# Ranks of a batch's tokens inside a Mixture-of-Experts router: sums along the tiles by VectorE's shifted additions, not by seven identity products on TensorE

## The reference

```python
logits = x @ wr.T                                  # x: 16384 tokens, 8 experts
vals, idx = jax.lax.top_k(logits, 2)
cap = int((T * 2 // E) * 1.25)                     # 5120
mask = (idx[:, :, None] == jnp.arange(E)).any(axis=1)
pos = jnp.cumsum(mask.astype(jnp.int32), axis=0) - 1   # rank of a token with its expert
keep = mask & (pos < cap)
slot = jnp.where(keep, pos, cap)
dispatch[e, slot] = token                          # then gather, two matmuls per expert, weighted sum
```

## Time and profile before

| What | Value |
|---|---|
| Median of 3 runs | 2128.93 us (2125.66 to 2129.43) |
| The profiled execution | 2128.42 us |
| Its span, from the first to the last instruction | 2126.7 us |
| Mean granted TensorE clock | 0.979 |
| Busy share of the span: PE, DVE, ACT, POOL | 95%, 70%, 58%, 59% |
| Runs of `rank` in the profile | 16, from 81.24 to 551.50 us |

### The profile page before, as it was taken

The page is one execution under the profiler, slowest core; times in us unless marked ns, Lnnn a source line. Parts: engine busy times, 40 slices in busy tenths (PEclk is TensorE's granted clock), DMA queues, the critical chain, the costliest instruction groups (busy, mean ns, idle before and its releaser), DMA issues.

```text
span 2126.7 us, 51586 instructions
## 1 busy us (share of the span) xinstructions
PE 2012.0 (95%) x16208; PEld 1954.1 (92%) x16209; DVE 1484.2 (70%) x4388; ACT 1228.6 (58%) x2775; POOL 1258.0 (59%) x1336
## 2 busy tenths in 40 slices
PE   6999999998269999999999999999999999999997
PEld 5988888887169999999999999999999999999997
DVE  3777887877447667667667767676677676666666
ACT  3566666666345656555656566555556565655654
POOL 1277667776745556565555565466565555655655
PEclk9999999999579999999999999999999999999999
DMA  5234334332222112111211211131131212211221
GB/s 184 80 131 147 126 130 149 121 124 101 71 97 89 42 41 90 50 51 38 89 55 47 96 54 53 47 103 57 53 103 60 65 58 67 66 61 62 74 69 58
DMA packets 102434, 173.11 MB, mean 81 GB/s; under 512 B 26499, under 2 KB 70622, under 8 KB 102256
## 3 DMA queue, kind: packets, MB, share of 16 engines
q0 software_dynamic: 45584, 84.59, 13.0%
q1 hardware_dynamic: 56800, 88.00, 12.1%
HBM read 121.41 MB, written 69.21 MB: 90 GB/s over the span
## 4 chain that ended last, share of the span: by engine, by line
PE 59%; issue 6%; POOL 3%; DVE 2%; DMA 1%; DVEq 1%; POOLq 0%
PE y_ps L1383 29%; PE h_ps L1367 27%; PE tb_ps L1348 2%; POOL rows L1099 1%; DMA out<-y,put_idx 1%; POOL base L1112 1%; POOL rstd_b L1105 1%; POOL out L1120 1%; DVE h_lo L1292 0%; DVE y_raw L1239 0%; DVE y L1272 0%; DVEq L1047 0%; DVEq L1048 0%; DVE w_hi L1309 0%; DVE stats_b L1250 0%
## 5 line engine op out<-in xcount | busy, mean ns | idle before, releaser
L1193 ACT ACTIVATE h_ps<-h_ps,b_sb 128x256 f32<-128x256 f32 x1032 | 415.8, 445 | 595.3 <-PE h_ps L1367 595.3
L1383 PE MATMUL y_ps<-w_hi,h_hi 128*128 128x256 f32 x2064 | 590.0, 286 | 8.5 <-DVE h_lo L1292 8.1
L1367 PE MATMUL h_ps<-bt_hi,w_hi 128*128 128x256 f32 x2064 | 573.4, 278 | 3.4 <-issue 2.0
L1383 PE MATMUL y_ps<-w_hi,h_lo 128*128 128x256 f32 x2064 | 575.9, 279 | 0.0
L1383 PE MATMUL y_ps<-w_lo,h_hi 128*128 128x256 f32 x2064 | 575.4, 279 | 0.0
L1367 PE MATMUL h_ps<-bt_lo,w_hi 128*128 128x256 f32 x2064 | 572.1, 277 | 0.0
L1367 PE MATMUL h_ps<-bt_hi,w_lo 128*128 128x256 f32 x2064 | 571.9, 277 | 0.0
L1383 PEld LDWEIGHTS y_ps<-w_hi,h_hi 128*128 128x128 f32 x2064 | 389.9, 189 | 14.8 <-DVE h_lo L1292 14.5
L1367 PEld LDWEIGHTS h_ps<-bt_hi,w_hi 128*128 128x128 f32 x2064 | 389.2, 189 | 5.2 <-issue 3.4
L1292 DVE TENSOR_TENSOR h_lo<-h_ps,h_hi 128x512 fp32r<-128x512 f32 x516 | 344.6, 682 | 66.8 <-ACT h_hi L1196 66.7
L1383 PEld LDWEIGHTS y_ps<-w_hi,h_lo 128*128 128x128 f32 x2064 | 389.3, 189 | 0.0
(11 more groups left out here) (211 smaller groups left out, 3404.9 us busy)
## 6 DMA issues: line engine op xcount, KB each, us to landing
xt_raw<-in_x_t SPq DMA_DIRECT2D x32, 512.0 KB
x_raw<-in_x SPq DMA_DIRECT2D x64, 256.0 KB, 3.2
w_raw<-in_w SPq DMA_DIRECT2D x16, 1024.0 KB
x_rows<-x_sb SPq DMA_DIRECT2D x32, 512.0 KB
out<-alone SPq DMA_DIRECT2D x32, 512.0 KB
rows<-x_rows,pick_idx POOLq DMA_INDIRECT x260
out<-y,put_idx POOLq DMA_INDIRECT x260, 2.5
base<-out,base_idx POOLq DMA_INDIRECT x258
```

Source lines behind the costliest of these rows:

```text
L1193: nc.scalar.activation(half, half, ACT.Gelu_apprx_tanh, bias=b1_sb[:, bass.ds(e * FT + 2 * g + i, 1)]).then_inc(gelu_done, 1)
L1367: ins = nc.tensor.matmul(h_ps[:, g, (f % 2) * BLK:(f % 2 + 1) * BLK], w[:, c:c + P], v[:, k, :], start=(i == 0), stop=(i == 3 * DK - 1))
L1383: ins = nc.tensor.matmul(y_ps[:, t, :], v[:, g, h:h + P], w[:, c:c + D], start=(f == 0 and t == 0 and part == 0), stop=(f == FT - 1 and t ...
```

## The change

The seven identity products are taken out of `rank`. VectorE instead sums the choices along the 8 tiles of a partition, by three additions at distances of 1, 2 and 4 tiles. The tile `chosen` has four planes with 4 zeroed tiles ahead of the 8 real ones, so that the shifted reads need no special case. The last tile of the last plane is the sum over all 8 tiles, which took a reduction before. A fourth new addition, `ahead_of`, adds the running slot numbers to the sums of the earlier tiles, and `ranked` adds TensorE's rank to that. GpSimd clears `chosen` once at the start, ahead of `minus_half`, and VectorE rounds two matrices to fp32r instead of three.

```diff
+            HEAD = 4
+            chosen = sb("chosen", [P, 4, HEAD + TILES, E])
+            ahead_of = sb("ahead_of", [P, TILES, E])
...
+                made(nc.gpsimd.memset(chosen[:, :, :, :], 0.0))
...
-                for src, dst in ((ident, ident_r), (tri_f, tri_r), (ones_f, ones_r)):
+                for src, dst in ((tri_f, tri_r), (ones_f, ones_r)):
...
-                ROUTE_STEPS = 25
+                ROUTE_STEPS = 28
...
-                        step(V.tensor_tensor(mask[:, :, :], pick[:, 0, :, :], pick[:, 1, :, :], ALU.add))
-                        step(V.tensor_reduce(mask_sum_f[:, :], mask[:, :, :].bitcast(F).rearrange("p t e -> p e t"), X, ALU.add))
-                        V.tensor_copy(mask_sum[:, :], mask_sum_f[:, :]).then_inc(mask_ready, 1)
+                        step(V.tensor_tensor(chosen[:, 0, HEAD:, :], pick[:, 0, :, :], pick[:, 1, :, :], ALU.add))
+                        for i in range(3):
+                            span = 1 << i
+                            step(V.tensor_tensor(chosen[:, i + 1, HEAD:, :], chosen[:, i, HEAD:, :],
+                                                 chosen[:, i, HEAD - span:HEAD - span + TILES, :], ALU.add))
+                        V.tensor_copy(mask_sum[:, :], chosen[:, 3, HEAD + TILES - 1, :]).then_inc(mask_ready, 1)
+                        step(V.tensor_tensor(ahead_of[:, :, :], chosen[:, 3, HEAD - 1:HEAD - 1 + TILES, :],
+                                             over_tiles(slot_next[:, :]), ALU.add))
                         step(V.tensor_tensor(gap[:, :], top[:, 1, :], top[:, 0, :], ALU.subtract))
...
-                        step(V.tensor_tensor(slot[:, :, :], rank_ps, over_tiles(slot_next[:, :]), ALU.add))
+                        step(V.tensor_tensor(slot[:, :, :], rank_ps, ahead_of[:, :, :], ALU.add))
...
-                    nc.tensor.matmul(rank_ps, tri_r[:, :], mask_sum[:, :].rearrange("p (a e) -> p a e", a=1).broadcast_to([P, TILES, E]),
-                                     start=True, stop=False)
-                    for t in range(TILES - 1):
-                        ins = nc.tensor.matmul(rank_ps[:, t + 1:TILES, :], ident_r[:, :],
-                                               mask[:, t:t + 1, :].broadcast_to([P, TILES - 1 - t, E]),
-                                               start=False, stop=(t == TILES - 2))
+                    ins = nc.tensor.matmul(rank_ps, tri_r[:, :], mask_sum[:, :].rearrange("p (a e) -> p a e", a=1).broadcast_to([P, TILES, E]),
+                                           start=True, stop=True)
```

More of the change, by code:

```diff
@@ L130, in build @@
             tri_f, ones_f = sb("tri_f", [P, P]), sb("ones_f", [P, P])
-            ident_r, tri_r, ones_r = sb("ident_r", [P, P], R), sb("tri_r", [P, P], R), sb("ones_r", [P, P], R)
+            tri_r, ones_r = sb("tri_r", [P, P], R), sb("ones_r", [P, P], R)
             second = sb("second", [P, TILES, E])
@@ L138, in build @@
             best = sb("best", [P, TILES])
-            mask = sb("mask", [P, TILES, E], R)
-            mask_sum_f, mask_sum = sb("mask_sum_f", [P, E]), sb("mask_sum", [P, E], R)
+            HEAD = 4
+            chosen = sb("chosen", [P, 4, HEAD + TILES, E])
+            ahead_of = sb("ahead_of", [P, TILES, E])
+            mask_sum = sb("mask_sum", [P, E], R)
             slot_next = sb("slot_next", [P, E])
@@ L988, in _ @@
                 ins.then_inc(wvo_ready, 1)
-                pe.wait_ge(r_split, 3)
+                pe.wait_ge(r_split, 2)
                 batches(pe, body)
```

## The result

The changed kernel takes 2131.41 us (median of 20 runs, 2129.04 to 2136.43), the kernel before 2127.61 us (20 runs, 2125.36 to 2130.84). The ratio is 1.0018, 95% interval 1.0012 to 1.0025: it is 3.8 us slower. I had forecast 2127.6 us, no difference, with a range of 2121 to 2131 us, and the time lies above it.

What follows compares the result with a forecast made beforehand. The prediction held a ScalarE and VectorE chain, not TensorE, to bound steady batches. From the profiled 2128.42 us it took 0.78 us for body 1 and nothing elsewhere: 2127.6 us, range 2121 to 2131 us.

Steps and rivals of the forecast that it cites:

- the cover: Bodies 2 to 14: a chain outside TensorE hides its saving; gain 0, without the cover 10.1 us.
- TensorE's own need of 31.25 us per batch: First stage: TensorE's work needs at most 31.25 us per batch, read from body 1, which has no `renormalize`.
- the chain of 31.7: Steady bodies: ScalarE and VectorE work from the last `kt` copy to `k_next(2)` sets the 31.7 us between ranks.
- three distances of the ranks: First stage: ranks 31.25 us apart in body 1, 31.45 in body 2, 31.7 later.
- one extra step of VectorE: In `address`, from body 3: a step of 0.207 us behind `g_lo` made every batch 0.2 us longer.
- slack: Steady batches: TensorE already has at least 0.45 us to spare per batch, 31.7 less 31.25.
- TensorE's new wait: Ahead of `attend(0)`: the saved 0.78 us turns into waiting for `qt_lo`, about 0.9 us in all.
- +0.48: VectorE ahead of the rank: three additions for one reduction delay `mask_ready` by 0.48 us, inside 1.07 us of slack.
- VectorE's 0.74 us more lies in what was a wait of 1.54 us. Cost 0: VectorE's routing ahead of `slot`: the added work fits an existing wait; cost 0, without that wait 9.6 us.
- VectorE as the bound by the additions' time: Between `q_maximum(1)` and `g_lo`: longer `choose` moves the chain, 2137.3 us, or 2135.4 if GpSimd holds an addition; chance 0.07.
- the clock: At `attend(0)`: added waiting drops TensorE to its lower clock, 18.7 us more, 2146.3 us; chance 0.03.
- The sum: Whole kernel: profiled 2128.42 us less 0.78 us from body 1, all other parts 0, gives 2127.6 us.

Runs made afterwards that it cites:

- e13: Changed kernel with twelve one-column clearings on VectorE ahead of its loop, moving the loop twelve places on; 2123.56 us, 0.9983 of the kernel before.
- e15: Changed kernel with twelve clearings ahead of VectorE's loop, second half of ScalarE's `renormalize` and `gate_exp` moved behind `g_hi`; 2108.18 us, 0.9911 of the kernel before.
- e16: Kernel before with 29 clearings behind VectorE's loop, second half of ScalarE's `renormalize` and `gate_exp` moved behind `g_hi`; 2119.76 us, ratio 0.9965.
- e3: Changed kernel with VectorE's loop over batch pairs written out, so it never jumps back; 2123.83 us, 0.9986 of the kernel before.
- e14: Kernel before with 29 one-column clearings on VectorE behind its first-stage loop, shifting its second-stage code; 2123.50 us, ratio 0.9984.
- e1: Kernel before with six one-column clearings per batch added to VectorE's loop, 266 instructions a pass; 2124.34 us, ratio 0.9992.
- e6: Kernel before with six clearings per batch in VectorE's loop and eight ahead, matching the changed loop's length and place; ratio 0.999 on a disturbed chip.

## Why the prediction was wrong

**Right: the cover.** TensorE's own need of 31.25 us per batch and the chain of 31.7 that hides a saving of 0.78 were read from three distances of the ranks and one extra step of VectorE. e13 (no gain) and e15 against e16 (11.6 us) show it. Body 1 gave 0.74 us where 0.78 were forecast (31.25 to 30.51). Two details were off. With the chain shortened the kernel before needs 31.33 to 31.39 us in bodies 3 to 13 (e16), so its slack was some 0.3 us per batch and not 0.45. And TensorE's new wait was to stand ahead of `attend(0)`, about 0.9 us on `qt_lo`; in e13 the larger part, 0.37, stands ahead of `q_next(3)`, for ScalarE's copy `x_raw`, and 0.21 ahead of `attend(0)`.

**Right: the durations.** The rank is 0.78 us cheaper at its identity products, and 0.86 in all. From the sum `chosen` to the copy `mask_sum` it is now 302.54 to 303.58, 1.04 us, and was 300.52 to 301.08, 0.56 us: +0.48, as summed. `slot` follows `scale_gap` at once, `g_lo` still follows `g_hi`, and TensorE's granted clock is 1.00 from 100 to 500 us. The new additions were not held by GpSimd either: three of them take 0.74 us together (302.80 to 303.54), although GpSimd's power instruction ran from 303.08 for 1.73 us.

**Wrong: the step "VectorE's 0.74 us more lies in what was a wait of 1.54 us. Cost 0".** It priced the additions by their time on the engine and left out their code. With their register instructions they add 12 instructions to a pass of the loop and 8 ahead of it. At that length and place each jump back stops VectorE for 3.3 to 4.2 us, of which 1.3 to 2.1 come through to the ranks: 7.05 us in four jumps, against 0 in the sum. With the loop twelve places on (e13) or written out (e3) they are gone, and the additions cost nothing. Neither the forecast nor a rival had this; my slower rivals, VectorE as the bound by the additions' time and the clock, are refuted by e3 and by the granted clock of 1.00 in the steady bodies.

**Missing: the second stage.** The sum took it as untouched. It is 5.4 us shorter in the profile. e14 shows that moving VectorE's code by the same 29 instructions does that alone: shorter stops, shorter waits of TensorE and a clock that falls for less time. In the medians the whole is 3.8 us slower: with 6.1 for the first stage that leaves about -2.3 for the second, a figure from one profile and two medians, so only its sign is firm.

**Too narrow: the range.** It was made from the prices of the parts, as if everything outside them stood still. The place of code alone moved the kernel before by 3.5 us (e14) and the changed one by 7 (the stops); a range of 10 us that ends 3.4 us above the forecast had no room for it.

Two things stay open. The steady distance is 31.71 to 31.84 us in e13 and e3 against 31.62 to 31.77 in e14, some 0.1 us per batch. A part of it lies at one step of `address`, for which I have no cause. And the exact limit of the place (the eight instructions between the end of e1's loop, which shows no stop, and that of the changed kernel's) was not narrowed down.

## What to carry to other kernels

Before an instruction is added to an engine's loop, count the instructions of a pass, register instructions for waits included, and after the edit compare the instruction queue's packets and the waits marked "issue" behind the jump back. No duration of an instruction shows this price. Judge a small edit by the stages of the profile, not by the total, since a shift of code can move a stage that has none of the changed lines by as much as the edit is worth. And when work is taken from a busy engine for no gain, look for the chain that it had to wait for anyway: here moving four activations and `gate_exp` made the same edit worth 11.6 us.

## What the runs showed of the hardware

- A jump back stopped VectorE for 3.3 to 4.2 us in the changed kernel, with four packets of 8 KB of the instruction queue in the first 8 us after it and a fifth some 34 us after it. The same jump without these packets showed no stop (e1, e13).
- A loop of 266 instructions on VectorE had no such packets at its old place (e1) and 20 places on (e13), and had them 8 places on (the changed kernel, e6).
- VectorE's two longest stops in the second stage, near 960 and 1360 us, are 5.8 and 5.0 us before and 4.3 and 4.5 in e14, with the code 29 instructions on. TensorE waits 3.4 and 2.7 us behind them before, 1.8 and 2.2 in e14.
- Behind the wait of 3.4 us TensorE's granted clock was 0.50 from 965 to 969 us, and its products of 256 columns started 0.21 us apart instead of 0.12.
- An instruction of VectorE with two inputs in SBUF took 0.23 us within a GpSimd instruction of 1.67 us. Three more took 0.74 us together, with one of 1.73 us running from the second on.
